# Decoder layer on one core: score and value products of a batch gathered into three groups over four PSUM banks

## The reference

```
h = x * rsqrt(mean(x^2) + 1e-6) * norm_w
q, k, v = h Wq^T, h Wk^T, h Wv^T            8 heads of 64; q and k are rotated
beta, ig, og = sigmoid(h W + b)             one number for each token and head
M_t = beta_t * M_(t-1) + ig_t / 8 * k_t v_t^T
y_t = og_t * (q_t M_t)
x1 = layernorm(x + y Wout^T + bout)
x2 = layernorm(x1 + x1 * r),   r_t = 0.9 r_(t-1) + ctx_t^2
out = layernorm(x2 + experts(x2))           8 experts, each 512 -> 2048 -> 512 with gelu
```

## Time and profile before

| what | value |
|---|---|
| median of 3 runs | 1248.84 us (1248.21 to 1250.78) |
| span of the profiled execution | 1250.1 us, all that the page gives of its own time |
| TensorE busy | 1230.2 us, 98% |
| VectorE / GpSimd / ScalarE busy | 62% / 59% / 37% |
| mean granted TensorE clock | 0.998 of full |
| DMA, mean | 144 GB/s; 53.3% of 16 engines |

### The profile page before, as it was taken

The page is one execution under the profiler, slowest core; times in us unless marked ns, Lnnn a source line. Parts: engine busy times, 40 slices in busy tenths (PEclk is TensorE's granted clock), DMA queues, the critical chain, the costliest instruction groups (busy, mean ns, idle before and its releaser), DMA issues.

```text
span 1250.1 us, 19325 instructions
## 1 busy us (share of the span) xinstructions
PE 1230.2 (98%) x6682; PEld 1011.4 (81%) x6682; DVE 780.7 (62%) x1297; ACT 460.8 (37%) x629; POOL 740.3 (59%) x519
## 2 busy tenths in 40 slices
PE   8989999999999999999999999999999999999998
PEld 7777888888888888778888888888888888888886
DVE  5887888888888888973544534543734535435424
ACT  5223333333233332353434434433534344343330
POOL 4876566666666666648538357274294385483651
PEclk9999999999999999999999999999999999999999
DMA  8778777777877776636307325235164073163310
GB/s 278 157 152 163 163 160 153 161 163 159 161 155 159 153 141 112 189 128 248 114 10 267 101 84 211 85 138 175 66 208 170 0 277 101 34 246 99 111 59 34
DMA packets 178107, 179.52 MB, mean 144 GB/s; under 512 B 44732, under 2 KB 121484, under 8 KB 178060
## 3 DMA queue, kind: packets, MB, share of 16 engines
q1 hardware_dynamic: 177548, 178.64, 53.3%
q10 hardware_dynamic: 512, 0.26, 0.1%
HBM read 137.55 MB, written 17.18 MB: 124 GB/s over the span
## 4 chain that ended last, share of the span: by engine, by line
PE 57%; DVE 2%; POOL 1%; issue 1%; DMA 0%; ACT 0%; POOLq 0%; DVEq 0%; ACTq 0%
PE qk_ps L89 5%; PE qk_ps L88 5%; PE qk_ps L87 5%; PE v_ps L87 5%; PE v_ps L89 5%; PE v_ps L88 5%; PE gate_ps L87 5%; PE gate_ps L89 5%; PE gate_ps L88 5%; PE s_ps L87 3%; PE s_ps L89 3%; PE s_ps L88 3%; PE y_ps L87 2%; PE y_ps L89 2%; PE y_ps L88 2%
## 5 line engine op out<-in xcount | busy, mean ns | idle before, releaser
L1006 POOL TENSOR_TENSOR w_lo<-w_raw,w_hi 128x2048 fp32r<-128x2048 f32 x31 | 143.2, 4620 | 97.8 <-ACT w_hi L760 97.8
L1342 DVE CAST hid_hi<-gate_ps 128x512 fp32r<-128x512 f32 x62 | 42.8, 690 | 193.6 <-ACT gate_ps L800 187.5
L998 POOL TENSOR_TENSOR w_lo<-w_raw,w_hi 128x2048 fp32r<-128x2048 f32 x32 | 147.7, 4617 | 12.3 <-ACT w_hi L770 12.3
L87 PE MATMUL qk_ps<-xT_parts,wqkv_hi 128*128 128x256 f32 x512 | 149.4, 292 | 2.4 <-ACT c_both L688 1.5
L1088 DVE TENSOR_TENSOR_SCAN decays<-f_all,diag 128x384 f32<-128x384 f32 x128 | 149.3, 1204 | 0.6
L88 PE MATMUL qk_ps<-xT_parts,wqkv_hi 128*128 128x256 f32 x512 | 145.4, 284 | 0.0
L89 PE MATMUL qk_ps<-xT_parts,wqkv_lo 128*128 128x256 f32 x512 | 145.2, 284 | 0.0
L1342 DVE CAST hid_hi<-v_ps 128x512 fp32r<-128x512 f32 x62 | 42.8, 690 | 141.2 <-ACT v_ps L800 141.2
L800 ACT ACTIVATE v_ps<-v_ps,b_cols 128x512 f32<-128x512 f32 x64 | 42.3, 662 | 191.0 <-PE v_ps L89 190.6
L87 PEld LDWEIGHTS qk_ps<-xT_parts,wqkv_hi 128*128 128x128 f32 x512 | 98.4, 192 | 13.3 <-issue 7.9
L800 ACT ACTIVATE gate_ps<-gate_ps,b_cols 128x512 f32<-128x512 f32 x64 | 42.2, 659 | 171.2 <-PE gate_ps L89 170.2
(11 more groups left out here) (238 smaller groups left out, 3220.9 us busy)
## 6 DMA issues: line engine op xcount, KB each, us to landing
w_raw<-in_w SPq DMA_DIRECT2D x64, 1024.0 KB, 7.7
f_all<-f_dram SPq DMA_DIRECT2D x16, 1024.0 KB, 4.9
qkT<-rot SPq DMA_DIRECT2D x256, 64.0 KB, 2.0
xT_raw<-in_xT SPq DMA_DIRECT2D x16, 512.0 KB, 12.7
x_both<-in_x SPq DMA_DIRECT2D x16, 512.0 KB, 11.5
f_all<-f_dram SPq DMA_DIRECT2D x16, 512.0 KB, 6.0
c_both<-in_ctx_in SPq DMA_DIRECT2D x16, 512.0 KB, 13.4
x_both<-x_dram SPq DMA_DIRECT2D x8, 1024.0 KB, 5.0
```

What stands on the lines that cost most here:

```text
L87: eng.matmul(out, lhs_hi, rhs_hi, start=first, stop=False)
L998: pool.tensor_tensor(w2_lo[s % 2][:], w2_raw[s % 2][:], w2_hi[s % 2][:].bitcast(F32), ALU.subtract)\
L1006: pool.tensor_tensor(w1_lo[s % 2][:], w1_raw[s % 2][:], w1_hi[s % 2][:].bitcast(F32), ALU.subtract)\
L1342: dve.tensor_copy(high, up_ps[c % 2][:]).then_inc(hid_hi_done, 1)
```

## The change

1. One PSUM tensor `score_ps` of four banks replaces `turn`, `s_ps` and `gate_ps`; banks 0 and 1 are the old `turn`, bank 2 is `s_ps` and bank 3 is `gate_ps`. For batches 1 to 14 (`in_fours`), odd pairs write their scores to banks 2 and 3.
2. For these batches, `attend` places the products in three groups: scores of pairs 0 and 1 behind share 4; values of pairs 0 and 1 and then scores of pairs 2 and 3 behind share 10; values of pairs 2 and 3 behind share 21. Batches 0 and 15 keep the old order.
3. Pairs 0 and 1 put their values into the two halves of `y_ps`, pairs 2 and 3 into those of `s_ps`. `y_high` and `y_low` take two pairs at a time (512 columns), twice for a batch.
4. `weigh_pair` weighs a pair with one instruction of 768 columns.
5. `middle` on DVE starts with `add_memory` and `norm_stats` and then weighs pairs 0 and 1; pairs 2 and 3 are weighed together after the first two scans.
6. Waits: scores of pair 1 wait for the residual of the batch before (bank 2) and for `sum_gates` (bank 3); the values of pair 2 wait for all four pairs' weighing; `project_out` waits for two `y_low`, not four.

```diff
-    turn = [bank(f"turn{n}") for n in range(2)]
+    score_ps = bank("score_ps", 2048)
+    score_banks = score_ps[:].rearrange("p (n c) -> p n c", c=D)
+    turn = [score_banks[:, n, :] for n in range(2)]
+    s_ps, gate_ps = score_banks[:, 2, :], score_banks[:, 3, :]
...
+    def in_fours(b):
+        return b.i is not None or 1 <= b.n <= B - 2
+
+    def pair_banks(b, c):
+        n = c % 2 * 2 if in_fours(b) else 0
+        return score_banks[:, n:n + 2, 0:DW]
...
+                if in_fours(b):
+                    if c == 1:
+                        pe.wait_ge(res_done, (b - 1).after(NT, NT))
+                        pe.wait_ge(gates_added, (b + 1).after(1, 1))
+                    elif c >= 2:
+                        pe.wait_ge(probs_done, b.after(KC, c - 1))
+                elif c >= 1:
+                    pe.wait_ge(probs_done, b.after(KC, c))
...
+            def attend(b, g):
+                if g == 4:
+                    scores(b, 0)
+                    scores(b, 1)
+                elif g == 10:
+                    weighted_values(b, 0)
+                    weighted_values(b, 1)
+                    scores(b, 2)
+                    scores(b, 3)
+                elif g == 21:
+                    weighted_values(b, 2)
+                    weighted_values(b, 3)
...
+                n = c % 2 * 2
+                dve.tensor_tensor(probs[:, n:n + 2, :], pair_banks(b, c), decays[:, 2 * c:2 * c + 2, :],
+                                  ALU.mult).then_inc(probs_done, 1)
...
             def middle(b, last):
-                weigh_pair(b - 1, 0)
                 add_memory(b - 2)
                 norm_stats(b - 2, 1)
+                weigh_pair(b - 1, 0)
                 weigh_pair(b - 1, 1)
                 rope_parts(b, 0)
-                y_low(b - 1, 0)
                 rope_parts(b, 1)
                 clear_f(b)
                 scans(b, 0, 1)
                 weigh_pair(b - 1, 2)
+                weigh_pair(b - 1, 3)
                 token_gates(b)
                 gate_v(b, 0)
+                y_low(b - 1, 0)
...
-                y_low(b - 1, 1)
                 scans(b, 2, 3)
                 if not last:
                     scans(b, 4, 5)
-                weigh_pair(b - 1, 3)
                 rope_parts(b, 2)
-                y_low(b - 1, 2)
                 rope_parts(b, 3)
                 scans(b, 4 if last else 6)
-                y_low(b - 1, 3)
+                y_low(b - 1, 1)
```

More of the change, by code:

```diff
@@ L642, in weights_high, with y_high @@
                         act.activation(wout_hi[:, k, :], wout_raw[:, k, :], ACT.Copy).then_inc(w_hi, 1)
-            def y_high(b, c):
-                act.wait_ge(y_mm, b.after(KC, c + 1))
-                if b.n >= 1 and c == 0:
+            def y_high(b, i):
+                act.wait_ge(y_mm, b.after(KC, 2 * i + 2))
+                if b.n >= 1 and i == 0:
                     act.wait_ge(out_mm, (b - 1).after(NT, NT))
-                act.activation(yT_hi[:, c, :], value_bank(b, c)[:, 0:L], ACT.Copy).then_inc(y_hi_done, 1)
+                act.activation(yT_hi[:, 2 * i:2 * i + 2, :], value_bank(i)[:].rearrange("p (c t) -> p c t", t=L),
+                               ACT.Copy).then_inc(y_hi_done, 1)
             def gate_low(b):
@@ L711, in body @@
                 for c in range(KC):
-                    if (b - 1).within(B):
-                        y_high(b - 1, c)
+                    if (b - 1).within(B) and c % 2:
+                        y_high(b - 1, c // 2)
                     if b.n == 1 and c == 0:
@@ L1491, in scores @@
                 if c == 0 and b.n >= 1:
-                    pe.wait_ge(probs_done, (b - 1).after(NH, NH))
-                if c >= 1:
-                    pe.wait_ge(probs_done, b.after(NH, 2 * c))
-                halves = (slice(0, DH), slice(DH, 2 * DH))
-                for rows, bank in zip(halves, score_banks(b)):
-                    pe.matmul(bank[:, 0:P], kT[rows, c, P:L], qT[rows, c, P:L], start=True, stop=True)
-                for rows, bank in zip(halves, score_banks(b)):
-                    pe.matmul(bank[:, P:DW], kT[rows, c, 0:P], qT[rows, c, 0:L], start=True, stop=True).then_inc(s_mm, 1)
+                    pe.wait_ge(probs_done, (b - 1).after(KC, KC))
+                if in_fours(b):
[6 more added lines that the diff above has]
+                    pe.wait_ge(probs_done, b.after(KC, c))
+                halves = (slice(0, DH), slice(DH, 2 * DH))
+                into = pair_banks(b, c)
+                for n, rows in enumerate(halves):
+                    pe.matmul(into[:, n, 0:P], kT[rows, c, P:L], qT[rows, c, P:L], start=True, stop=True)
+                for n, rows in enumerate(halves):
+                    mm = pe.matmul(into[:, n, P:DW], kT[rows, c, 0:P], qT[rows, c, 0:L], start=True, stop=True)
+                mm.then_inc(s_mm, 1)
             def weighted_values(b, c):
-                if c >= 2:
-                    pe.wait_ge(y_lo_done, b.after(KC, c - 1))
-                elif c == 0 and b.n >= 1:
+                if c == 0 and b.n >= 1:
                     pe.wait_ge(res_done, (b - 1).after(NT, NT))
-                y = value_bank(b, c)
+                pe.wait_ge(probs_done, b.after(KC, KC if c == 2 and in_fours(b) else c + 1))
+                y = value_bank(c // 2)[:, c % 2 * L:(c % 2 + 1) * L]
                 v = v_sb[b.odd]
-                pe.wait_ge(probs_done, b.after(NH, 2 * c + 2))
                 for n in (2 * c, 2 * c + 1):
@@ L1549, in project_out @@
                     if j == 0:
[L1550 removed]
+                        pe.wait_ge(y_lo_done, b.after(2, 1))
                     for k in range(KC):
[L1552 to L1553 removed]
+                        if j == 0 and k == 2:
+                            pe.wait_ge(y_lo_done, b.after(2, 2))
                         tok = slice(j * P, (j + 1) * P)
@@ L1576, in body @@
             def body(b):
-                for n in range(NH):
-                    slot(b, n)
+                if b.within(B) and in_fours(b - 1):
+                    for g in range(3 * NH):
+                        project_share(b, g)
+                        attend(b - 1, g)
+                else:
+                    for n in range(NH):
+                        slot(b, n)
                 if b.n == B:
```

49 lines of the change are left out of this document (18 added, 31 removed).

## The result

| | before | after |
|---|---|---|
| median | 1249.81 us (4 runs, 1248.21 to 1251.42) | 1236.83 us (4 runs, 1234.79 to 1238.27) |
| ratio, 95% interval | | 0.9902 [0.9885, 0.9920] |
| span of the profiled execution | 1250.1 us | 1236.5 us |
| ten steps, per step | 32.37 us | 31.35 us |

The kernel became 1.0% faster, by 13.0 us in the medians and 13.6 us between the two spans. The forecast for the median was 1235.5 with a range of 1232.6 to 1242.5, and the forecast for the span 1236.8.

A forecast was written before the change was run, and what follows sets the result against it. TensorE's own work was taken as the bound in attention. Fewer form changes save 14.7 us, the last steps return 1.4: 13.3 us off, span 1236.8, median 1235.5, range 1232.6 to 1242.5.

The forecast's parts named there:

- The bound: Steps 2 to 14: TensorE's own work, busy 392.2 of 394.0 us; DVE, at 85%, is the second limit.
- The cost of a change of form: TensorE in attention: three groups for five cost 1.29 us, not 2.34; 1.05 less in each of 14 batches.
- Values to scores: TensorE's middle group: going from value to score products, not seen before, takes 0.21 us, between 0.10 and 0.40.
- Only the gap is saved: TensorE's form changes: first loads stay open, or value to score products cost 0.40; gain 7.0 us, 1241.8; chance 0.10.
- The ends: Last pairs in steps 15 and 16: products wait for shared y_high and y_low; 0.3 and 1.1 us go back.
- The starting steps: Steps up to 3: no term of their own, only the 1.05 us less for each of batches 1 to 14.
- +23.0. So the slack grows to 1.4 us: DVE ends rope_parts 3 at +23.0 of the step, TensorE reaches cross_memory at +24.4; slack 1.4 us.
- `rope_parts` 3 done over 1 us ahead of `cross_memory`: Sign in the trace after the change: DVE ends rope_parts 3 over 1 us before TensorE's cross_memory.
- The third rival, DVE as the bound: DVE's scans, stretched against POOL's work, delay cross_memory: 1245.3 us, up to 1273.3; slower had chance 0.05.
- moves forward along with the scans: Argument against DVE becoming the bound: POOL's work following the second layernorm shifts earlier with DVE's scans; no size given.
- With weighing left between, the waits would stay and DVE would come at +24.7: DVE's order: weighing left between keeps the waits for scores; rope_parts 3 ends at +24.7, TensorE comes at +24.4.
- 14.7 - 1.4 = 13.3: Whole kernel: 14.7 us gained over batches 1 to 14, less 1.4 us in the last steps, gives 13.3 us.

The follow-up runs named there:

- three splits: The changed kernel with scores 0 and 1 apart, middle-group values and scores alternating, or values 2 and 3 apart: 0.9937, 0.9942, 0.9934 of before.
- ctx narrow: The changed kernel with POOL's low part of ctx cut to 32 of 512 columns in the loop's steps: 1239.84 us, one run.
- both edits: The changed kernel with weighing of pair 0 ahead of the second layernorm and POOL's low part of ctx cut to 32 of 512 columns: 1256.97 us.
- pairs only: The changed kernel with the old order on TensorE and DVE, keeping weighing by pairs and two-pair y_high and y_low: 1253.06 us, 1.0005 of before.

## Why the prediction was right

**The bound.** Right. TensorE's own work set the time in the steps before and after, and the gain came out of its busy time.

**The cost of a change of form.** Right in kind, a few per cent too large. The forecast was 1.05 us a step and 1.02 came; over 14 batches 14.2 in place of 14.7 us. The three splits say where: one cost 0.37 for a summed 0.40, one 0.32 for 0.36, one 0.32 for 0.34. Each term read off a few rows is some 0.01 to 0.02 high, about the spacing of the trace's last digit. Values to scores, the term without a row, measured the 0.21 taken. *Only the gap is saved* is excluded by these runs.

**The ends.** 1.4 us was forecast and about 1.8 came, 1.1 in step 16 and after, as worked out, and 0.7 in step 15 for 0.3. The product that had to wait was the right one.

**The starting steps.** The forecast moved nothing there beyond a normal step, and the execution gained 0.8 us more: 2.9 by step 3, where steps 2 and 3 owed 2.0. One wait and a fall of the clock went, two other waits came. In the nine profiles with the new order on DVE the output of step 2 started between 95.96 and 99.09 us and that of step 3 between 128.50 and 133.39, and of before there is one profile. So 0.8 us is far inside what these steps vary by, and is not put down to the change.

**DVE.** This is where the right number rested on a wrong step. The step was "+23.0. So the slack grows to 1.4 us". It summed what DVE loses in waits and instructions and left the rest where it was, with the stretched scans at the 2.98 us that they had. Moved 1.2 us earlier, the first met most of a 2.37 us instruction of POOL, and the two took 4.18; `add_memory` took 0.55 more, and the four later scans 0.75 less. The slack came out at 0.2 us, and that it is not below zero is luck; the sign given for it, "`rope_parts` 3 done over 1 us ahead of `cross_memory`", did not come. The third rival, DVE as the bound, was that near. Its mechanism, POOL holding the scans, is shown, but it had four more scans stretched where two were hit harder and later ones got freer. What was held against it, that POOL's work "moves forward along with the scans", was wrong: POOL's instruction stayed at +9.6.

**The price of the cover.** "With weighing left between, the waits would stay and DVE would come at +24.7" priced the edit at 0.3 us a step. It was 1.91. The forecast kept the old waits of 0.40 and 1.25 for it, but the edit itself puts the scores three shares later, so the wait to use was 2.40, and the slack behind it was the 0.2 us above.

**The end figure.** 14.7 - 1.4 = 13.3 was forecast. What came was 14.2 - 1.8 + 1.1 = 13.5 (the 1.1 are 0.8 up to step 3 and 0.3 in step 14), beside 13.6 between the spans. Errors of 0.4 to 1.1 us with different signs stand behind an agreement of 0.3 us, and the change's second profile differs from the first by 2.6 us at step 3 and by 1.6 us in the stretch to step 16. The agreement to 0.3 us is luck; the step of 31.35 us for a forecast of 31.3 is not.

**Left open.** Why POOL stood still for 5.8 us in one execution, and whether it was a late transfer. Whether the slow first piece is its weight load. Whether the second scan would be free as well with `o_tables` elsewhere, and what that would buy if DVE's order were then tightened: it was not tried.

## What to carry to other kernels

Where the busiest engine shows no idle time, read its timeline from start to start: in this kernel each way out of a TensorE tile form and back costs 0.32 to 0.37 us, and putting products of one form side by side saves that without removing any work. Before a step of the second-busiest engine is moved, lay the third engine's instructions under its new place: here a scan took 0.96 or 2.28 us by what POOL did then, and one line in DVE's order decided between 1.0% faster and 1.2% slower. When work is merged in pairs to save instructions, look at the last one of the program: it makes the first half wait for the second.

## What was unexpected of the hardware

- How long a scan of the same size takes depends on the POOL instruction beside it: 2.28 us under one of 2.37, 0.96 with that one cut to 0.32. The scan is held to the end of that instruction: at six places read (the first two scans of the step shown, before and after, the second with ctx narrow, and the second of the two with both edits) it ended 0.81 us after it.
- A wait can cost the clock too, and does not always. Step 2 has a wait for `qkT` of 3.1 us before and of 2.7 us in the kernel with pairs only; both show a granted clock of 0.79 from 72 to 80 us, and the other eleven profiles, which have no such wait there, 1.00. But the same wait of 1.9 us in step 15 of the same kernel left the clock at 1.00 in one execution and brought 3 us at 0.50 in another, which cost 1.6 us.
- Of the twelve profiled executions of the change and its variants three lost time at a place where the same code lost none in other steps or another execution: 3.7 us with POOL idle for 5.8 us, 0.7 us with late work of ACT, and 1.6 us by the clock. A single profile of such a kernel can be off by as much as the edit under test.
